# Attention pass: a block's late node work moved from the block's border into the edge groups of the next round

## The reference

```
x = layernorm(x + attention(x))        # h = x@W, 4 heads; per edge leaky_relu(a_src[src] + a_dst[dst]);
                                       # softmax over the edges of a target, weighted sum of h[src]; @ Wl + bl
x = layernorm(x + std_of_neighbours(x))
x = layernorm(x + gine(x, edge_attr))  # sum of x[src] + edge_attr@We, then a two-layer MLP
x = layernorm(x + sage4(x))            # four mean aggregations with weights
```

## Time and profile before

| | before |
|---|---|
| median of 3 runs | 9799.77 us (9795.94 to 9801.96) |
| the profiled execution | 9789.83 us, span 9788.2 us |
| busy: TensorE | 6498.4 us, 66% |
| busy: VectorE | 4539.3 us, 46% |
| busy: GpSimd | 4718.8 us, 48% |
| busy: ScalarE | 1864.8 us, 19% |
| mean granted TensorE clock | 0.834 |

### The profile page before, as it was taken

How to read it: one execution, slowest core, us unless ns; L and a number is a source line. 1 busy time by engine, 2 the same in 40 slices (tenths; PEclk the granted TensorE clock), 3 DMA queues, 4 the chain that set the end, 5 groups by cost and what they waited for, 6 DMA issues and landing times.

```text
span 9788.2 us, 254659 instructions
## 1 busy us (share of the span) xinstructions
PE 6498.4 (66%) x65048; PEld 4741.4 (48%) x65049; DVE 4539.3 (46%) x11895; ACT 1864.8 (19%) x3800; POOL 4718.8 (48%) x4467
## 2 busy tenths in 40 slices
PE   4888777777726666665778866675776455455676
PEld 3666555555512221112444555664675454454566
DVE  4555555555578877774443333332222232232333
ACT  1433333333311334552000000000000000000000
POOL 2777666565500000004762036544764775774765
PEclk7888888888868889998889987887888677677788
DMA  2444444443310112334566566675776677677676
GB/s 56 100 97 95 94 91 94 92 89 87 87 33 39 79 80 116 131 138 171 174 185 191 177 221 203 221 230 172 226 253 209 208 276 266 207 259 243 211 268 231
DMA packets 973391, 1566.40 MB, mean 160 GB/s; under 512 B 499841, under 2 KB 621441, under 8 KB 966402
## 3 DMA queue, kind: packets, MB, share of 16 engines
q1 hardware_dynamic: 485762, 1244.14, 36.9%
q0 software_dynamic: 150016, 196.43, 9.7%
q10 hardware_dynamic: 337280, 122.87, 4.8%
HBM read 1337.91 MB, written 225.00 MB: 160 GB/s over the span
## 4 chain that ended last, share of the span: by engine, by line
PE 33%; issue 22%; DVE 15%; DVEq 11%; POOL 10%; DMA 7%; ACT 2%; ACTq 1%; SPq 0%; POOLq 0%
PE ps_turn L999 15%; POOL ARENA L671 10%; PE ps_turn L954 5%; PE ps_out L844 4%; DMA ARENA<-edge_attr 3%; DMA ARENA<-counts 2%; DVE ARENA L1886 2%; DVE ARENA L1884 2%; PE ps_pair L844 2%; PE ps_turn L817 1%; PE ps_pair L1021 1%; DVEq L1891 1%; DVEq L1981 1%; DVE ARENA L1981 1%; DVE DSUM L2050 1%
## 5 line engine op out<-in xcount | busy, mean ns | idle before, releaser
L999 PE MATMUL ps_turn<-ARENA 128*128 128x192 bf16 (+2 forms) x28812 | 2810.5, 267 | 834.6 <-DVE DSUM L2050 397.0
L999 PEld LDWEIGHTS ps_turn<-ARENA 128*128 128x128 bf16 x28812 | 2355.8, 108 | 1297.4 <-issue 996.4
L671 POOL DMA_INDIRECT ARENA<-table_sage,idx x1920 | 2013.1, 1048 | 1143.4 <-issue 963.6
L671 POOL DMA_INDIRECT ARENA<-table_gat,idx x1568 | 1693.8, 1080 | 851.9 <-issue 480.0
L954 PE MATMUL ps_turn<-ARENA 128*128 128x392 bf16 (+1 forms) x4204 | 1063.8, 359 | 679.7 <-DVE ARENA L1886 407.0
L671 POOL DMA_INDIRECT ARENA<-table_dev,idx x480 | 492.2, 1025 | 1616.6 <-ACT idx L1220 1472.3
L1884 DVE TENSOR_SCALAR ARENA<-ARENA 128x784 bf16<-128x784 f16 (+1 forms) x2102 | 1009.2, 480 | 363.5 <-issue 238.1
L954 PEld LDWEIGHTS ps_turn<-ARENA 128*128 128x128 bf16 (+1 forms) x4204 | 335.6, 101 | 1407.7 <-issue 1364.8
L671 POOL DMA_INDIRECT ARENA<-table_gine,idx x480 | 500.9, 1043 | 847.1 <-issue 684.0
L1202 ACT ACTIVATE ARENA<-ps_turn 128x784 f32 x784 | 645.9, 824 | 1086.4 <-PE ps_turn L954 1086.1
L2050 DVE TENSOR_REDUCE DSUM<-ps_turn 128x64 f32<-128x192 f32 (+2 forms) x686 | 263.9, 385 | 1171.7 <-PE ps_turn L999 966.3
(11 more groups left out here) (320 smaller groups left out, 5616.5 us busy)
## 6 DMA issues: line engine op xcount, KB each, us to landing
ARENA<-counts SPq DMA_DIRECT2D x1764, 448.0 KB
counts<-ARENA SPq DMA_DIRECT2D x49, 3136.0 KB, 9.0
ARENA<-counts SPq DMA_DIRECT2D x588, 224.0 KB
ARENA<-dst_b SPq DMA_DIRECT2D x393, 256.0 KB
ARENA<-edge_attr ACTq DMA_DIRECT2D x392, 128.0 KB
ARENA<-table_sage,idx POOLq DMA_INDIRECT x1920
ARENA<-table_gat,idx POOLq DMA_INDIRECT x1568
nodes_dev<-table_rows ACTq DMA_DIRECT2D x14, 672.0 KB
```

What stands on the lines that cost most here:

```text
L671: pool.indirect_dma_start(ps["buf"][:, s, c, 0:ps["row"]], None, ps["table"][:, :], bass.IndirectOffsetOnAxis(idx[:, s, c:c + 1], 0)).then ...
L999: last = pe.matmul(ps_dense[half][:, 0:n], RING[:, b, :], XP[:, b, :], start=(b == PIECE_AT[pieces[0]]), stop=(j == pieces[-1] and b == PI ...
```

## The change

The late half of a block is no longer done at the next border but in the first round after its own border, spread over the slots of that round. A register on each engine, `owed`, is 1 from a border until the engine has done its part:

- TensorE: the product stands in front of slot 1 (behind the sums of slot 0), its output is now the start of ps_turn.
- VectorE: the 14 steps are cut into four pieces, behind slots 2, 3, 5 and 6 (4, 4, 4 and 2 steps).
- ScalarE: the root stands behind slot 4's work, the casts and stores behind slot 7's.
- Each place is in an If on `owed`, so that every round passes it and only the first after a border enters it. If a block had no round at all, the border would still do the owed half.
- y moves from tmp (used inside the round for one-hots) to a part of `big`, and `gat_normalise` waits for one more release of its rows, as the late half of block b - 1 now ends ahead of it.

```diff
+PRODUCT_AT, MEAN_AT, SPREAD_AT, ROOT_AT, NORM_AT, PARTS_AT, ROWS_AT = 1, 2, 3, 4, 5, 6, 7
-        ps_gat = ps_exp_all[:, 64:64 + TB * D]
+        ps_gat = ps_turn[:, 0:TB * D]
...
+        def owes(eng, owed):
+            return eng.If(eng.snap(owed, min_val=0, max_val=1) > 0)
+
+        def sweep(eng, one_round, finish, dense, late, owed):
+
+            eng.reg_mov(owed, 0)
...
-                if late is None:
-                    dense(b)
-                else:
-                    dense(b, lambda: late_half(eng, b, late))
-            if late is not None:
-                late(BLOCKS - 1)
...
+                with owes(eng, owed):
+                    late(nc.s_assert_within(b - 1, 0, BLOCKS - 1, skip_runtime_bounds_check_because="a block is owed, so b > 0"))
+                    settle(eng)
+                dense(b)
+                eng.reg_mov(owed, 1)
+            late(BLOCKS - 1)
...
# TensorE
-                def one_round(i):
+                def one_round(i, before):
                     for s in range(SLOTS):
                         g = i * SLOTS + s
+                        if s == PRODUCT_AT:
+                            with owes(pe, owed):
+                                gat_product(pe, before)
+                                pe.reg_mov(owed, 0)
...
# ScalarE
                     act.activation(onehots[:, s % 2, :], distance, ACT.Relu, scale=-1.0, bias=ONE[:, :]).then_inc(passes[0]["first_hot"], 1)
+                    if s == ROOT_AT:
+                        with owes(act, owed):
+                            node_root(0, before)
+                    if s == ROWS_AT:
+                        with owes(act, owed):
+                            node_rows(0, before, before)
+                            act.reg_mov(owed, 0)
...
-            def gat_copy(b, late):
-                late()
+            def gat_copy(b):
...
# VectorE: the 14 steps, by piece
+                y = view(big[:, TB * 2 * D:], D)
                 both = view(big, 2 * D)
+                if 0 in pieces:
+                    step.n = 0
+                    ve.wait_ge(step_sem["product"], block_count("product", ps["name"], b))
+                    ve.wait_ge(old_x_loaded, b * 16 + 16)
+                    step(ve.tensor_tensor(y, view(ps_gat, D), old_x, ALU.add))
+                    ve.sem_inc(product_read, 1)
+                    step(ve.tensor_tensor(y, y, row(CV[:, :]), ALU.add))
+                    take_mean(y)
+                if 1 in pieces:
+                    step.n = 4
+                    take_spread(y)
+                if 2 in pieces:
+                    step.n = 8
+                    norm_to(b, y, xb)
+                    step(same(both[:, :, 0:D], xb))
+                    step(ve.tensor_tensor(both[:, :, D:2 * D], xb, xb, ALU.mult))
+                if 3 in pieces:
+                    step.n = 12
+                    store_parts(2 * D)
...
-            ve.wait_ge(rows_free, b + 1)
+            ve.wait_ge(rows_free, b + 2)
...
                         sum_last(s, g, *last_span(ve, spans, s), i * 2 + (s // 4 + 1))
+                        for piece, at in enumerate((MEAN_AT, SPREAD_AT, NORM_AT, PARTS_AT)):
+                            if s == at:
+                                with owes(ve, owed):
+                                    late_step.start(before, LATE_STEPS)
+                                    node_vector(ve, late_step, k, split, before, before, pieces=(piece,))
+                                    settle(ve)
+                                    if piece == 3:
+                                        ve.reg_mov(owed, 0)
```

More of the change, by code:

```diff
@@ L925, in pass_tensor, with dense @@
                 last.then_inc(ps["first_agg"], 1)
-                def dense(b, late=None):
-                    if late:
-                        late()
+                def dense(b):
                     node_tensor(pe, k, b)
@@ L937, in finish @@
                     further_tiles(SLOTS - 1, *span(pe, spans[3]))
-                sweep(pe, one_round, finish, dense,
-                      (lambda b: gat_product(pe, b)) if gat else None)
+                sweep(pe, one_round, finish, dense, lambda b: gat_product(pe, b), owed)
             def build_tensor():
@@ L1123, in _, with one_round @@
             act.activation(WSELF[:, :, :], WSELF[:, :, :], ACT.Exp).then_inc(self_exp, 1)
-            def one_round(i):
+            owed = act.alloc_register("act_owed")
+            def one_round(i, before):
                 for s in range(SLOTS):
@@ L1269, in _ @@
                 if k == 0:
-                    sweep(act, one_round, lambda: None, gat_copy, lambda b: node_scalar(0, b, b))
+                    sweep(act, one_round, lambda: None, gat_copy, lambda b: node_scalar(0, b, b), owed)
                     build_scalar()
@@ L1294, in same, with node_vector @@
             return nc.vector.tensor_scalar(dst, src, 1.0, None, ALU.mult)
-        def node_vector(ve, step, k, split, b, blk, head=True, tail=True):
+        def node_vector(ve, step, k, split, b, blk, head=True, tail=True, pieces=range(4)):
             ps = passes[k]
@@ L1343, in node_vector @@
                 xb = a[:, :, 0:D]
[L1344 to L1349, removed]
-                both = view(big, 2 * D)
[L1351 to L1356, removed]
+                y = view(big[:, TB * 2 * D:], D)
+                both = view(big, 2 * D)
+                if 0 in pieces:
[5 more added lines that the diff above has]
+                    step(ve.tensor_tensor(y, y, row(CV[:, :]), ALU.add))
+                    take_mean(y)
+                if 1 in pieces:
+                    step.n = 4
+                    take_spread(y)
+                if 2 in pieces:
[6 more added lines that the diff above has]
+                    store_parts(2 * D)
             if name == "dev":
@@ L1803, in pass_vector, with dense @@
                 per = node_steps[name]
-                def dense(b, late_half=None):
+                def dense(b):
                     step.loop(b, per)
[L1807 to L1811, removed]
+                    gat_normalise(ve, step, b)
                 def late(b):
@@ L1816, in late @@
                     assert late_step.n == late_step.per
-                sweep(ve, one_round, finish, dense, late if gat else None)
+                sweep(ve, one_round, finish, dense, late, owed)
                 step.close(BLOCKS)
```

34 lines of the change are left out of this document (19 added, 15 removed).

## The result

The changed kernel takes 9886.99 us (9872.85 to 9898.71), the kernel before, beside it on the same chip, 9800.86 us: a ratio of 1.0086 [1.0069, 1.0104], 86 us more. The profiled execution took 9898.71 us with a span of 9896.9. The forecast was 9790, the range 9735 to 9855.

A forecast was written before the change was run, and what follows sets the result against it. The prediction took the attention pass as a ring of VectorE, ScalarE, an edge DMA and TensorE, none saturated. 192 - 162 - 20 = 10 us less than 9789.83 gave 9780, plus 9.94 to the runs' median: 9790, range 9735 to 9855.

The forecast's parts named there:

- What leaves the border, 13 x 14.8 = 192: At thirteen borders, TensorE's gap falls from 25.85 to 11.1 us, 14.8 us less each, 192 us gross.
- What comes into the round, 12.5 x 13 = 162: In the first round after each border, moved work costs 11 us plus 1.5 for TensorE's clock, 162 us over thirteen.
- the walk: Slot-by-slot reckoning of the round after border 1: 12.2 us of inserted work makes its end 11 us later.
- owed rounds over 58 us: First rounds after a border longer than 58 us, with granted clock below 0.8, would point to rival 2; 54 to 57 expected.
- rival 2: Slots 1, 2, 3, 5, 6 of owed rounds: ring pays in full, TensorE's clock falls; 59 us more, 9859; chance 0.14.
- rival 4: At the borders: no shrinking, because something else takes 25 us there; 9982 us; chance 0.03.
- Conditions, 20 us (0 to 60): In all 49 rounds, four more Ifs on VectorE at 0.25 us each, nearly half showing: 20 us.
- The table load in every round, hidden: On ScalarE before slot 5's Exp, one 1.28 us load in all 49 rounds, hidden by a 2.29 us wait: cost 0.
- Casts and stores covered by the way back: ScalarE's slot 7 work, 6.1 us, nearly all covered by VectorE's 4.98 us return; uncovered, 65 us come back.
- Rival 3: TensorE's grown loop no longer stays: 3.2 us more per border, 42 us, 9832; 157 us if each round; chance 0.06.
- my -10: The whole kernel's forecast change: 192 us gained, less 162 in the rounds and 20 for conditions, 10 us less.

The follow-up runs named there:

- kernel with the copy first: The kernel before, with ScalarE's copy of the turned block put ahead of the previous block's root, casts and stores at the border: 9784.10 us, 0.9975.
- kernel without the dead copy: The changed kernel with the never-entered spare copy of the product taken out of TensorE's loop at the border: 9819.87 us, 1.0011.
- without the stores: The kernel without the dead copy, with ScalarE's three row stores of each block issued together behind the last block: 9812.02 us, 1.0008.

## Why the prediction was wrong

Step by step, in its order:

- *What leaves the border, 13 x 14.8 = 192.* Too large. The thirteen borders, measured on VectorE, give back 148 us, and the passage behind the last score step 10 in the traces (59.6 to 49.5 us). Together 158. The 14.8 was TensorE's gap. On VectorE, from the last normalising step to the next score step, the twelve later borders took 19.9 us as a mean and take 6.5 without the late half (border 0 had 6.8), which is 13.3 less; about 1 us of it is lost again ahead of the normalising. The kernel with the copy first shows that TensorE's idle time was in part no one's loss. That gap, without the refetch, is 13.0 us and not 11.1.
- *What comes into the round, 12.5 x 13 = 162.* Nearly right up to the last slot. In the kernel without the dead copy, in the round that I walked and counted from its first score step, groups 2, 3, 4, 6 and 7 (the first is 0) start 2.4, 5.8, 7.0, 9.8 and 11.9 us later than before, against 2.5, 4.8, 6.2, 8.5 and 10.7 in the walk, and the first rounds grew by 12.3 us each over their seven slot periods, 160 in all. What it left out is the round's end: the next round starts 14.8 us later and not 11, and the ways out of the twelve owed rounds that another follows grew by 34 us. They fell back by 33 without the stores. VectorE's slow load of the group bounds is 22 of it, in ten of the twelve. The prediction had this load at the border and counted it as gone. Of the 12.3, the pieces are 5.1 to 7.7 and the product 2 to 3, in whichever place it stands. The prediction's own sign of error, owed rounds over 58 us, came true (62.7, and 59.0 without the refetch), but not for rival 2's reason: the granted clock there was 0.82, not below 0.8, and the pieces were not paid in full. Its sign for rival 4, a border over 15 us, came true by the fetch: 17.2 us as a mean with it.
- *Conditions, 20 us (0 to 60).* 36 to 39 by the times, inside its ends; in the traces the other rounds of the kernel without the dead copy grew by 5 us and the ways out of them by 11, together 16.
- *The table load in every round, hidden.* Right: one in each of the 49 rounds of the changed kernel, and 49 more cost no time that shows.
- *Casts and stores covered by the way back.* This step failed too: ScalarE's work was covered, but its transfers were not. VectorE's load of the bounds met them (34 us, as said above).
- *Rival 3, instruction fetch, 0.06 and 42 us.* This is the step that failed most, 73 of the 96 us: the sum takes TensorE's loop as one that stays and has nothing for its fetch. "Its loop grows by 28 matmuls with their weight loads; if it no longer stays, the border costs 3.2 more": it no longer stays, and the border costs 3.4 at the one shown. Border and slot 0 together cost 4.2 us as a mean in the traces and 5.6 by the times (73 us, in the changed kernel and in the kernel before alike). I priced it by one stop of VectorE's, and gave it 0.06 because I had no count of how near TensorE's loop was to its limit. The eight fetches of the earlier trace rows say that it stayed; they don't say by how much.

Sum without the refetch, by the traces: -158 + 160 + 34 + 16 = 52 us more. From the first score step to the first step behind the pass that kernel is 53 us longer, 35 in its span, as later parts that nothing changed are 18 shorter in this execution, and 11 [1, 21] by the times. The traced execution of the kernel before lay 11 us below its median and this one 5.5 above its own; without these the 35 would be 19, which the interval holds. So the 52 is the account of one fast and one slower execution, and 11 is what the change costs without the refetch. By the times, my -10 was 21 us off in what I had reckoned with and 73 in what I had called unlikely, together near the 96 between forecast and result. In the traces the two misses of the sum go the same way, a gain 34 us too high and a round's end of 34 left out.

The Trainium skill, page Runtime: NRT & Kernel Launch, section Instruction fetch mechanics, says that TensorE's instruction memory has 128 KiB, is a first-in-first-out store and is refilled in blocks of 16 KiB. The trace agrees on the block, 0.15 MB in nine fetches at border 1. An estimate from that page's figures: nine such blocks are 144 KiB, more than that memory, and a loop of nine blocks in it would be fetched whole each time round, which fits the lots of nine. Neither the size nor the length of the loop is measured by a run here.

## What to carry to other kernels

- Before code is added to a loop, count the instructions of the engine's whole loop and look at the fetches in its instruction queue: none during the loop says that it stays, not how much room is left. Here code that is never entered cost as much as code that is, 73 us either way. Duplicate a piece of work only where there is room.
- Take what a border costs on the engine that the next group waits for. An idle time on another engine may be no one's loss.
- When work is moved, its transfers move too. Ask what stands behind them in the same queue, and which loads of registers run beside them.
- Measure a round from its first step to the first step of the next: the way out of it, 11.4 us here, is a part of it.

## What the runs showed of the hardware

- TensorE's instruction queue fetched 7 or 8 times 16 KB in the pass, or 125 times, for 56 more matmuls and weight loads in a loop; with 24 of them, 60 times, in lots of nine at six of thirteen borders. The lot cost the first slot behind the border 4.2 us as a mean, the later slots nothing that shows.
- A load of ten registers from SBUF by VectorE's sequencer took 1.08 us, and 2.6 to 3.95 us beside 1.5 MB of ScalarE's stores (12 of 98 loads in the kernel before, 10 in the changed one, none where the stores stood at the end).
- A 128 KB load issued behind such stores by the same engine kept TensorE waiting up to 7.3 us; in the kernel before 1.9 us was the longest such wait.
- The same 28 matmuls took 3.23 us, and 6.20 us at the granted clock of 0.50, behind 4.00 us of TensorE's idle time at a border.
